# Second layer's gate moved from TensorE's last row set to VectorE in the feed-forward of an adaptive layer-norm block

## The chip, the cores and the metric

The kernel runs on one core of a Trainium2 chip. The metric is the device time of one execution in microseconds (us), the median of several runs. A core has five engines that work side by side and wait for one another through semaphores: TensorE (PE, matrix products; PEld are its weight loads), VectorE (DVE), ScalarE (ACT), GpSimd (POOL) and SyncE (SP, which here only starts DMA transfers; SPq and ACTq are the queues of SP and ACT).

## The reference

```python
x = L0_attn_data                                    # 2 batches x 512 rows x 512
mod = (_silu(L0_c) @ L0_wmod).reshape(2, 6, 1, -1)  # c: 2 x 512, wmod: 512 x 3072
sa, ca, ga, sb, cb, gb = (mod[:, 0], mod[:, 1], mod[:, 2], mod[:, 3], mod[:, 4], mod[:, 5])
ga = (2 * (ga >= 0) - 1) * jnp.maximum(jnp.abs(ga), 0.25)
gb = (2 * (gb >= 0) - 1) * jnp.maximum(jnp.abs(gb), 0.25)
h = _layernorm(x, axis=-1) * (1 + ca) + sa
x = x + ga * _L0_attn_ref(h, weight, mask)          # h @ (weight * block mask).T, 512 -> 512
h = _layernorm(x, axis=-1) * (1 + cb) + sb
x = x + gb * _L0_ffn_ref(h, Wg, Wu, Wd, ag, au, ad) # silu(h Wg.T * ag) * (h Wu.T * au), Wd.T, * ad; 512 -> 1376 -> 512
return x
```

The six vectors of `mod` (a shift, a scale and a gate for each of two layers, per batch) come from one small product with a 512 x 3072 matrix. The change is about the last of them, `gb`, the gate of the feed-forward.

## The kernel before

Everything is written out by hand: each engine has its own instruction stream, whose order is the order in the code, with a semaphore for every hand-over. The 1024 rows of x are 8 tiles of 128 rows (`n = 4 * b + t`, batch b, tile t).

**First layer.** VectorE takes means and variances of the tiles and normalises them; TensorE transposes them (`transposes`), ScalarE applies scale and shift (`modulate(n)`, n = 0..7), and TensorE multiplies with the masked weights: `linear(b, k, t)`, 32 products in all, k the inner quarter. The block mask is summed by VectorE (`sum_mask(k)`), spread by a small product (`mask_blocks(k)`), turned to 0/1 (`keep_blocks(k)`) and applied by GpSimd. Batch 1 of the first layer is normalised into a layout from which DMA moves (`move_first`, and `keep_in_place` for the blocks that stay) and VectorE's 32 x 32 transposes make the turned tiles.

**The modulation vectors** come in four sets, `rows_first`, `rows_second`, `rows_third`, `rows_last`. Each set (`mod_rows`) is a row of small products of `silu(c)` with weights in `modw`; ScalarE copies the result (`copy_rows`), TensorE turns it (`columns(n)`), and VectorE sums the columns out of the bank (`mod_columns`, `gate_sums`). The last set holds shift and scale of the second layer (slots 0 and 1 of `modw`) and the gate `gb` (slot 2). It stands in TensorE's stream behind `linear(1, 1, 1)`. Behind it stand the rest of the linears and `transposes(8)` to `transposes(11)`, which turn batch 0 of the second layer; `modulate(8)` to `modulate(11)` on ScalarE and `split` on VectorE make of each the high and low part that the feed-forward multiplies.

**Feed-forward.** It has STEPS = 22 steps, s = 0..21: 11 chunks of 128 inner features for batch 0, then the same for batch 1. A step has 16 products on TensorE (`gate_up(s)`, L935), a silu on ScalarE (L504), three operations on VectorE (`ffn_inner(s)`, L698, L705, L707) and 8 products (`down(s)`, L1005) two steps later. ScalarE also rounds each chunk's weights and, in the first steps, checks each chunk (`check_chunk(c)`, L442: is the low half of its words zero?). The results of the checks, in three groups of chunks, choose one of two product forms: `flag_vector(g)` on VectorE waits for the checks of group g, `flag_sum(g)` on TensorE adds them up, `read_flag(g)` brings the flag to a register. `flag_sum(2)` stands in TensorE's stream behind `gate_up(6)`, ahead of `down(4)`; `flag_vector(2)` stands on VectorE at the start of step 6. In steps 0 to 2 VectorE also normalises batch 1 of the second layer (`stats`, `normalise(3)`); 16 DMA moves and, in steps 5 to 8, `transpose_blocks` turn it.

**SP's queue** holds nearly all loads in one order: x, mask, weights of the first layer and the modulation, then the second layer's shift and scale (L294, L298, L300), its gate (L301, 1 MB), and then the chunks of the feed-forward, two transfers each (L308, L309). Chunks 0 to 3 follow at once; chunks 4 to 7 wait for `modulate(7)`; chunks 8 to 10 (from H1_CHUNK on) wait for the last linear, since their space holds the first layer's h.

**The second gate** before: `guard_gate(1)` in step 3 works on eight columns that `gate_sums(1)` took out of the bank, scales them with the down scale, and SP writes the turned line to DRAM and spreads it from there to all partitions (L324). It is wanted by `gate_ffn(0, 0)` on VectorE, when `down(10)` has made its first tile.

Of the kernel before, what the change touches and what calls it, by code (L numbers as in the profile page):

```python
# [25 lines left out]
ALU = mybir.AluOpType  # L26
# [4 lines left out]
P = 128  # L31
D = 512
KT = D // P
NB = 2
# [42 lines left out]
def adaln_block(nc, x, att_w, att_mask, cond, mod_ln1, mod_ln2, mod_gate, w_gu, w_gu_tail, w_down,  # L77
                scales, scales_tail, down_scale, out):
    with ExitStack() as ctx:
# [22 lines left out]
        gcol = sb("gcol", [P, 2, KT, NB])  # L102
        gscr = sb("gscr", [P, 2, KT, NB])
        gfin = sb("gfin", [P, 2, BLK])
        gturn = sb("gturn", [P, 2, BLK])
# [9 lines left out]
        colv = sb("colv", [P, 2, KT, NB])  # L115
# [69 lines left out]
        gcol_ok = sem("gcol_ok")  # L185
        gate_done = sem("gate_done")
        gate_ok = sem("gate_ok")
        gturn_ok = sem("gturn_ok")
        d_line = [sem(f"d_line{layer}") for layer in range(2)]
# [59 lines left out]
        def store_gate(eng, layer):  # L249

            eng.wait_ge(gturn_ok, layer + 1)
            line = gate_line[layer].rearrange("b k i -> (b k) i")
            for g in range(GRP):
                eng.dma_start(line[:, g * BLK:(g + 1) * BLK], gturn[BLK * g:BLK * g + NB * KT, layer, :])\
                   .then_inc(d_line[layer], 16)
# [5 lines left out]
        def _(sp):  # L261
# [59 lines left out]
            store_gate(sp, 1)  # L321
            sp.wait_ge(d_line[1], 16 * GRP)
# [61 lines left out]
        def _(act):  # L384
# [67 lines left out]
            def round_d(s):  # L452
# [22 lines left out]
            store_gate(act, 0)  # L475
# [5 lines left out]
               .then_inc(d_gate_first, 16)  # L481
            copy_rows(3)
            check_chunk(next(check_at))
# [39 lines left out]
        def _(dve):  # L523
# [3 lines left out]
            dve.memset(gfin[:, :, :], 0.0).then_inc(zeroed, 1)  # L527
# [98 lines left out]
            def gate_sums(layer):  # L626

                sum_columns(SETS - 2 + layer, bank[3 if layer else 7], GATE_AT, KT,
                            colv[:, layer, :, :].rearrange("p i b -> p (i b)")).then_inc(cols_ok, 1)
# [11 lines left out]
            def guard_gate(layer):  # L641


                dve.wait_ge(cols_ok, layer + 1)
                g = colv[:, layer, :, :]
                half_sign, gate = gscr[:, layer, :, :], gcol[:, layer, :, :]
                by_batch = gfin[:, layer, 0:NB * KT].rearrange("p (b k) -> p k b", b=NB)
# [7 lines left out]
                if layer == 0:  # L655
                    dve.wait_ge(zeroed, 4)
# [80 lines left out]
            for j in range(GRP):  # L737
                keep_in_place(j)
# [442 lines left out]
```

## Time and profile before

| | |
|---|---|
| median of 3 runs | 175.96 us (175.79 to 176.62) |
| the profiled execution | 176.29 us, span 174.5 us |
| mean granted TensorE clock | 0.999 |
| TensorE busy | 167.5 us, 96% |
| VectorE busy | 102.6 us, 59% |
| ScalarE busy | 80.9 us, 46% |
| GpSimd busy | 27.7 us, 16% |

The span reaches from the first to the last instruction of the profile; 1.79 us of the execution lie around it. Times in the profile are us from the span's start. A row of the timeline merges neighbouring instructions of one kind: its start, how long they took together, their number, and in brackets the idle time ahead of them with what ended it. One fp32 product with 512 columns stands as two records (two passes), one with 128 columns too, so the 48 products of `rows_last` are x96. A transfer's landing is its issue time plus the time to landing.

### The profile page before, as it was taken

The page shows a single profiled execution, that of the slowest core. Times are in us where ns is not written, and L with a number is a line of the kernel's source. Part 1 is how long each engine was busy: PE and PEld are TensorE (multiplying, and loading weights), DVE is VectorE, ACT ScalarE, POOL GpSimd, SP SyncE. Part 2 cuts the span into 40 slices and gives each one's busy share as a digit, 9 for nine tenths or more (in the row PEclk, how much of TensorE's full clock was granted, in tenths as well). Part 3 has the DMA queues.
Part 4 walks back from the last instruction along what each step waited for, and adds up shares of the span by engine and source line. Part 5 has one row for each costly group of instructions (what it writes and reads, how often), then busy time and mean ns, then how long its engine had stood idle before and what let it go on. Part 6 is the DMA issues. An engine that isn't in the chain of part 4 may idle for free.

```text
span 174.5 us, 2549 instructions
## 1 busy us (share of the span) xinstructions
PE 167.5 (96%) x892; PEld 128.4 (74%) x892; DVE 102.6 (59%) x216; ACT 80.9 (46%) x113; POOL 27.7 (16%) x32
## 2 busy tenths in 40 slices
PE   6889999979999999999999999999999999999992
PEld 6855554455468888888888888888888888888781
DVE  6778966990783999414855554437544313442574
ACT  3034005508999958755466442553425534252200
POOL 1233321930039310000000000007400000000000
PEclk9999999999999999999999999999999999999999
DMA  5999976999999501443000000001500000000014
GB/s 168 359 407 401 405 212 185 411 405 355 414 389 337 159 0 34 103 95 114 29 0 4 0 4 0 4 0 62 184 4 0 4 0 4 2 4 0 4 60 180
DMA packets 12789, 23.99 MB, mean 138 GB/s; under 512 B 3072, under 2 KB 5376, under 8 KB 12384
## 3 DMA queue, kind: packets, MB, share of 16 engines
q1 hardware_dynamic: 11056, 22.03, 35.1%
q10 hardware_dynamic: 1712, 1.66, 3.1%
q8 instruction: 16, 0.26, 0.6%
q14 instruction: 5, 0.04, 0.1%
HBM read 19.74 MB, written 2.11 MB: 125 GB/s over the span
## 4 chain that ended last, share of the span: by engine, by line
PE 80%; DMA 8%; DVE 5%; SPq 4%; issue 1%; ACT 0%; ACTq 0%
PE bank L935 46%; PE bank L1005 20%; PE bank L906 8%; DMA modw<-in_mod_gate 5%; DMA xt<-in_x 3%; SPq L246 3%; PE bank L813 2%; PE bank L991 2%; PE bank L885 2%; DVE wffn L576 1%; DVE xn L556 1%; DVE bns L542 1%; DVE xt L803 0%; SPq L263 0%; DVE xn L717 0%
## 5 line engine op out<-in xcount | busy, mean ns | idle before, releaser
L935 PE MATMUL bank<-ht,whi_gu 128*128 128x512 f32 x352 | 83.5, 391 | 0.0
L935 PEld LDWEIGHTS bank<-ht,whi_gu 128*128 128x128 f32 x352 | 65.6, 188 | 13.7 <-issue 0.5
L698 DVE SCALAR_TENSOR_TENSOR awork<-bank,scal,awork 128x512 f32<-128x512 f32 x22 | 16.5, 750 | 50.9 <-PE bank L935 47.6
L1005 PE MATMUL bank<-whi_dn,in_split 128*128 128x512 f32 x148 | 37.2, 391 | 0.0
L504 ACT ACTIVATE awork<-bank,scal 128x512 f32<-128x512 f32 x22 | 15.2, 689 | 45.3 <-PE bank L935 45.3
L1005 PEld LDWEIGHTS bank<-whi_dn,in_split 128*128 128x128 f32 x148 | 27.6, 188 | 6.0
L906 PE MATMUL bank<-awork,wffn 128*128 128x512 f32 x64 | 30.5, 603 | 0.2 <-ACT wffn L427 0.2
L449 ACT ACTIVATE whi_gu<-wffn 128x1024 fp32r<-128x1024 f32 x22 | 23.3, 1058 | 6.6 <-PE bank L935 6.6
L906 PEld LDWEIGHTS bank<-awork,wffn 128*128 128x128 f32 x64 | 11.0, 190 | 10.3 <-issue 9.0
L707 DVE TENSOR_TENSOR in_split<-awork,in_split 128x512 fp32r<-128x512 f32 x21 | 16.5, 785 | 0.7
L442 ACT ACTIVATE junk<-wffn 128x1536 uint8<-128x1536 uint16 x11 | 16.2, 1476 | 0.2
L379 POOL TENSOR_TENSOR xt<-xt,xn 128x512 f32<-128x512 f32 x4 | 5.2, 1346 | 54.5 <-DVE xn L717 54.5
L457 ACT ACTIVATE whi_dn<-wffn 128x512 fp32r<-128x512 f32 x21 | 13.1, 622 | 0.0
L542 DVE BATCH_NORM_STATS2 bns<-xt 128x6 f32<-128x512 f32 x16 | 10.8, 674 | 1.6 <-DMA xt<-in_x 1.5
L358 POOL TENSOR_TENSOR xt<-xt,xn 128x512 f32<-128x512 f32 x8 | 10.2, 1308 | 3.6 <-DVE xn L676 3.6
L402 ACT ACTIVATE rows<-bank,onerow 128x128 f32<-128x128 f32 x4 | 1.5, 368 | 19.9 <-PE bank L813 19.9
L705 DVE CAST in_split<-awork 128x512 fp32r<-128x512 f32 x21 | 9.0, 430 | 0.7
L345 POOL TENSOR_TENSOR rstd<-veps,mhalf 128x2 f32<-128x2 f32 x8 | 6.1, 763 | 15.2 <-DVE veps L547 15.1
L1074 PE MATMUL bank<-ident 128*128 128x128 f32 x34 | 6.6, 382 | 1.6 <-POOL ident L338 1.6
L1074 PEld LDWEIGHTS bank<-ident 128*128 128x128 f32 x34 | 6.4, 293 | 1.6 <-POOL ident L338 1.6
L813 PEld LDWEIGHTS bank<-modw,sc 128*32 128x32 f32 x192 | 5.0, 110 | 3.2 <-issue 3.2
L813 PE MATMUL bank<-modw,sc 128*32 128x128 f32 x192 | 6.1, 274 | 0.9 <-DMA modw<-in_mod_gate 0.9
(75 smaller groups left out, 109.6 us busy)
## 6 DMA issues: line engine op xcount, KB each, us to landing
wffn<-in_w_gu SPq DMA_DIRECT2D x10, 512.0 KB, 11.7
modw<-in_mod_ln SPq DMA_DIRECT2D x6, 512.0 KB, 7.1
wffn<-in_w_down SPq DMA_DIRECT2D x10, 256.0 KB, 13.1
xt<-in_x SPq DMA_DIRECT2D x8, 256.0 KB, 6.3
modw<-in_mod_gate SPq DMA_DIRECT2D x2, 1024.0 KB, 10.2
maskt<-in_att_mask SPq DMA_DIRECT2D x4, 256.0 KB, 8.0
awork<-in_att_w SPq DMA_DIRECT2D x4, 256.0 KB, 8.1
modw<-in_mod_ln SPq DMA_DIRECT2D x1, 1024.0 KB, 6.7
```

The lines of the kernel that those rows point to most:

```text
L442: act.activation(junk[:, :], low, ACT.Copy, accum_out=chk[:, c:c + 1])\
L449: act.activation(whi_gu[:, s % 2, :], wffn[:, s % C, 0:2 * D], ACT.Copy)\
L457: act.activation(whi_d(s), raw_d(s % C), ACT.Copy).then_inc(wd_hi, 1)
L504: act.activation(silu_g[:, s % 2, :], bank[gu_bank(s, 0)][:, :], ACT.Silu, scale=scal[:, s % C, 0:1]).then_inc(silu_ok, 1)
L542: dve.bn_stats(bns[:, q, t, :], xt[:, n % (NB * TT), :]).then_inc(bn_done, 1)
L698: dve.scalar_tensor_tensor(inner[:, s % 2, :], bank[gu_bank(s, 1)][:, :], scal[:, c, 1:2], silu_g[:, s % 2, :], ALU.mult, ALU.mult).then_i ...
L707: dve.tensor_tensor(lo, inner[:, s % 2, :], hi.bitcast(F32), ALU.subtract)\
L813: last = pe.matmul(dst[BLK * j:BLK * (j + 1), 0:P], sc[:, j, at * BLK:(at + 1) * BLK], source(j), start=(i == 0), stop=(i == len(blocks) - 1))
L906: last = pe.matmul(bank[4 * b + t][:, :], h1[:, b, k, t * P:(t + 1) * P], awork[:, k, :], start=(k == 0), stop=(k == KT - 1))
L935: return pe.matmul(bank[gu_bank(s, u)][:, :], w, h, start=(k == 0 and part == 0), stop=(k == KT - 1 and part == 1))
L1005: last = pe.matmul(bank[4 + t][:, :], h, w, start=(c == 0 and part == 0), stop=(c == C - 1 and part == 1))
L1074: pe.matmul(bank[0][:, 0:P], ident[:, :], ident[:, :], start=True, stop=True)
```

## The change

The gate `gb` leaves TensorE's last row set. Its 1 MB of weights is loaded behind the eighth chunk (chunk 7) instead of ahead of the first. VectorE makes the products itself in steps 3 and 4: for each batch one multiplication and three fused multiply-adds of 128 x 512 with a column of `silu(c)` (`second_gate_products`), turns them in step 5 with one 32 x 32 block transpose over 128 x 1024 and sums each block's row (`second_gate_sums`), and in step 9 folds the four partition groups together, guards, scales and turns the result (`guard_second_gate`, 14 small operations). SP stores one 32 x 32 line in one transfer instead of four. In TensorE's stream the last set has 32 products instead of 48, and `columns(3)`, the transposes 8 to 11 and `flag_sum(0)` stand one or a few linears earlier. On ScalarE one `check_chunk` moves from behind `copy_rows(3)` to ahead of it. On VectorE `sum_mask(3)` moves ahead of the four `keep_in_place`.

```diff
             sp.dma_start(modw[:, 1, :, :], mod_ln2[1]).then_inc(d_ln2[1], 16)
-            sp.dma_start(modw[:, 2, :, :], mod_gate[1]).then_inc(d_gate[1], 16)
...
                 if c == H1_CHUNK:
+                    sp.dma_start(modw[:, 2, :, :], mod_gate[1]).then_inc(d_gate[1], 16)
                     sp.wait_ge(att_done, NB * TT)
...
+            check_chunk(next(check_at))
             copy_rows(3)
             check_chunk(next(check_at))
-            check_chunk(next(check_at))
...
+            def second_gate_products(b):
+                dve.wait_ge(silu_c, 1)
+                dve.wait_ge(d_gate[1], 16)
+                for j in range(KT):
+                    w, c = modw[:, 2, j, :], sc[:, j, b:b + 1]
+                    if j == 0:
+                        dve.tensor_scalar(gates[:, b, :], w, c, None, ALU.mult).then_inc(gate2_part, 1)
+                    else:
+                        dve.wait_ge(gate2_part, KT * b + j)
+                        dve.scalar_tensor_tensor(gates[:, b, :], w, c, gates[:, b, :], ALU.mult, ALU.add)\
+                           .then_inc(gate2_part, 1)
+            def second_gate_sums():
+                dve.wait_ge(gate2_part, NB * KT)
+                turned = gates[:, NB:2 * NB, :].rearrange("p b n -> p (b n)")
+                dve.transpose(turned, gates[:, 0:NB, :].rearrange("p b n -> p (b n)")).then_inc(gate2_turned, 1)
+                dve.wait_ge(gate2_turned, 1)
+                dve.tensor_reduce(gsum[:, :], turned.rearrange("p (n i) -> p n i", i=BLK), AX_X, ALU.add)\
+                   .then_inc(gate2_sum, 1)
...
+            sum_mask(3)
             for j in range(GRP):
                 keep_in_place(j)
-            sum_mask(3)
...
             mod_columns(3)
-            gate_sums(1)
...
-                if s == 3:
-                    guard_gate(1)
+                if s in (3, 4):
+                    second_gate_products(s - 3)
                 if 5 <= s < 9:
                     transpose_blocks(s - 5)
+                if s == 5:
+                    second_gate_sums()
                 if 6 <= s < 10:
                     split(6 + s)
+                if s == 9:
+                    guard_second_gate()
...
-                pe.wait_ge(d_gate[1], 16)
                 pe.wait_ge(att_read, 3)
-                mod_rows([(KT * slot + i, modw_block(slot, i)) for slot in range(3) for i in range(KT)], bank[2])
+                mod_rows([(KT * slot + i, modw_block(slot, i)) for slot in range(2) for i in range(KT)], bank[2])
...
                     if (k, t) == (1, 1):
                         rows_last()
+                    if (k, t) == (1, 2):
+                        columns(SETS - 1)
                     if (k, t) == (1, 3):
-                        columns(SETS - 1)
-                    if (k, t) == (2, 0):
                         transposes(8)
                         transposes(9)
-                    if (k, t) == (2, 2):
+                    if (k, t) == (2, 0):
                         transposes(10)
                     if (k, t) == (2, 3):
                         transposes(11)
-                    if (k, t) == (3, 0):
                         pe.wait_ge(modc_ok, SETS)
                         flag_sum(0)
```

What the change makes of TensorE's stream between `linear(1, 1, 1)` and `flag_sum(0)` is seen in the next two lists. L906 and L980 are the linears, L813 and L888 the row set, L859 and L933 `columns(3)`, L885 and L959 the transposes 8 to 11. Before:

```order
L813 MATMUL bank<-modw,sc 32x128 [waits d_gate1,att_read,d_ln2_1,d_ln2_0]
L813 MATMUL bank<-modw,sc 32x128 x47
L906 MATMUL bank<-awork,wffn 128x512 x2
L859 MATMUL bank<-ident,rows 128x128 [waits att_read,rows_copied]
L906 MATMUL bank<-awork,wffn 128x512 [waits h_ok]
L885 MATMUL bank<-ident,xn 128x128 [waits att_read,xn_ok]
L885 MATMUL bank<-ident,xn 128x128 x3
L885 MATMUL bank<-ident,xn 128x128 [waits att_read]
L885 MATMUL bank<-ident,xn 128x128 x3
L906 MATMUL bank<-awork,wffn 128x512 x2
L885 MATMUL bank<-ident,xn 128x128 [waits h_ok]
```

And of the change:

```order
L888 MATMUL bank<-modw,sc 32x128 [waits att_read,d_ln2_1,d_ln2_0]
L888 MATMUL bank<-modw,sc 32x128 x31
L980 MATMUL bank<-awork,wffn 128x512
L933 MATMUL bank<-ident,rows 128x128 [waits att_read,rows_copied]
L980 MATMUL bank<-awork,wffn 128x512
L959 MATMUL bank<-ident,xn 128x128 [waits att_read,xn_ok]
L959 MATMUL bank<-ident,xn 128x128 x3
L959 MATMUL bank<-ident,xn 128x128 [waits att_read]
L959 MATMUL bank<-ident,xn 128x128 x3
L980 MATMUL bank<-awork,wffn 128x512 [waits h_ok]
L959 MATMUL bank<-ident,xn 128x128 [waits h_ok]
```

The wait for `d_gate1` and 16 products are gone; between the row set and `columns(3)` stands one linear instead of two, between it and the transposes 8 and 9 two instead of three, and between these and the transposes 10 one instead of two.

On ScalarE, around `copy_rows(3)` (L402, of the change L426), L442 and L466 are `check_chunk`, L430 and L454 `modulate`, L480 and L504 the spreading of the first gate. Before:

```order
L480 DMA maskt<-gate_line 128x512 [waits d_line0]
L402 ACTIVATE rows<-bank,onerow 128x128 [waits cols_done,rows_done]
L442 ACTIVATE junk,chk<-wffn 128x1536 [waits d_ffn0]
L442 ACTIVATE junk,chk<-wffn 128x1536 [waits checked,d_ffn1]
L430 ACTIVATE hbuf<-bank,modc 128x512 [waits modc_ok,xt_done] x2
```

And of the change:

```order
L504 DMA maskt<-gate_line 128x512 [waits d_line0]
L466 ACTIVATE junk,chk<-wffn 128x1536 [waits d_ffn0]
L426 ACTIVATE rows<-bank,onerow 128x128 [waits cols_done,rows_done]
L466 ACTIVATE junk,chk<-wffn 128x1536 [waits checked,d_ffn1]
L454 ACTIVATE hbuf<-bank,modc 128x512 [waits modc_ok,xt_done] x2
```

The check of chunk 0 now stands ahead of the copy, that of chunk 1 still ahead of `modulate(8)`.

On VectorE, the end of step 5 and the start of step 6, of the change (before, the rows L701 and L703 are not there, and L682 and L687 are the flag's two):

```order
L622 STREAM_TRANSPOSE xn<-modw 128x512 [waits d_blocks3,d_blocks2,xt_done,d_blocks1,d_blocks0]
L701 STREAM_TRANSPOSE maskt<-maskt 128x1024 [waits gate2_part]
L703 TENSOR_REDUCE gsum<-maskt 128x32 [waits gate2_turned]
L754 TENSOR_REDUCE flagv<-chk 128x1 [waits checked]
L759 TENSOR_SCALAR flags<-bank 1x1 [waits flag_done]
L770 SCALAR_TENSOR_TENSOR awork<-bank,scal,awork 128x512 [waits in_lo,silu_ok,up_mm]
```

Two operations over 1024 columns now stand between the block transpose of step 5 and `flag_vector(2)` (L754).

## Rows read from the trace of the kernel before

**Rows 1.** The page: busy time of TensorE.

```profile
PE 167.5 (96%) x892; PEld 128.4 (74%) x892; DVE 102.6 (59%) x216; ACT 80.9 (46%) x113; POOL 27.7 (16%) x32
```

**Rows 2.** The chain that ended last, in order of time: start, us, what.

```profile
27.86 8.81 DMA modw<-in_mod_gate
...
41.77 0.86 PE bank L906 x2
42.63 0.87 PE bank L885 x8
...
50.70 10.89 PE bank L935 x48
```

**Rows 3.** Timeline of TensorE from 32 to 66 us.

```profile
31.57 4.46 PE L906 MATMUL bank<-awork,wffn 128*128 128x512 f32 x10
36.91 2.83 PE L813 MATMUL bank<-modw,sc 128*32 128x128 f32 x96 [0.89 <-DMA modw<-in_mod_gate]
```

**Rows 4.** SP's timeline: when the transfers were issued.

```profile
10.36 0.43 SPq L266 DMA_DIRECT2D maskt<-in_att_mask  x1
...
27.35 0.46 SPq L300 DMA_DIRECT2D modw<-in_mod_ln  x1
...
29.12 0.68 SPq L309 DMA_DIRECT2D wffn<-in_w_down  x1
...
30.46 0.44 SPq L309 DMA_DIRECT2D wffn<-in_w_down  x1
```

**Rows 5.** DMA, one transfer each, last column us to landing; gate line last.

```profile
maskt<-in_att_mask SPq DMA_DIRECT2D x1, 256.0 KB, 12.2
modw<-in_mod_ln SPq DMA_DIRECT2D x1, 1024.0 KB, 6.7
wffn<-in_w_down SPq DMA_DIRECT2D x1, 256.0 KB, 9.5
wffn<-in_w_down SPq DMA_DIRECT2D x1, 256.0 KB, 11.1
maskt<-gate_line SPq DMA_DIRECT2D x1, 512.0 KB, 3.5
```

**Rows 6.** Timeline of all engines from 20 to 50 us.

```profile
21.91 1.77 DVE L582 COPY wffn<-wffn 32x512 f32<-32x512 f32 x4
23.71 0.69 DVE L603 TENSOR_REDUCE msum<-maskt 128x16 f32<-128x512 int32 x1
24.45 0.30 PEld L869 LDWEIGHTS bank<-msum,blkones 128*128 128x128 f32 x2 [0.29 <-DVE msum L603]
...
37.02 2.08 DVE L576 TENSOR_SCALAR xn<-xt,mv,rstd 128x512 f32<-128x512 f32 x4
39.80 0.37 ACT L402 ACTIVATE rows<-bank,onerow 128x128 f32<-128x128 f32 x1 [5.32 <-PE bank L813]
41.72 1.48 ACT L442 ACTIVATE junk<-wffn 128x1536 uint8<-128x1536 uint16 x1
43.20 1.43 ACT L430 ACTIVATE hbuf<-bank,modc 128x512 f32<-128x512 f32 x2
```

**Rows 7.** Timeline in the feed-forward, steps 0, 5 and 6.

```profile
56.24 1.67 DVE L707 TENSOR_TENSOR in_split<-awork,in_split 128x512 fp32r<-128x512 f32 x1
...
79.33 0.69 DVE L707 TENSOR_TENSOR in_split<-awork,in_split 128x512 fp32r<-128x512 f32 x1
79.94 0.71 DVE L598 STREAM_TRANSPOSE xn<-modw 128x512 f32<-128x512 f32 x1
80.57 0.12 DVE L682 TENSOR_REDUCE flagv<-chk 128x1 fp32r<-128x4 f32 x1
83.10 0.08 PEld L920 LDWEIGHTS bank<-onecol_r,flagv 128*1 128x1 f32 x1
```

**Rows 8.** One feed-forward step by windows: length, then each engine's busy time.

```profile
71.94:77.38 5.44, 5.44 (x25) 4.51 (x25) 1.87 (x3) 3.62 (x7) 0.00 (x0) 1.00 0.42 99
```

**Rows 9.** Groups of VectorE instructions by form: busy us, mean ns.

```profile
L665 DVE STREAM_TRANSPOSE gturn<-gfin 128x32 f32<-128x32 f32 x2 | 0.4, 213 | 0.1
```

More of the change, by code:

```diff
@@ L474, in _ @@
             modulate(4)
-            store_gate(act, 0)
+            store_first_gate(act)
             modulate(5)
@@ L658, in guard_gate @@
                    .then_inc(gate_m, 1)
-                dve.wait_ge(gate_m, layer + 1)
-                if layer == 1:
-                    dve.wait_ge(d_small, 48)
-                    dve.tensor_tensor(by_batch, gate, adc[:, :].unsqueeze(2).to_broadcast([P, KT, NB]),
-                                      ALU.mult).then_inc(gcol_ok, 1)
-                    dve.wait_ge(gcol_ok, 1)
-                dve.transpose(gturn[:, layer, :], gfin[:, layer, :]).then_inc(gturn_ok, 1)
+                dve.wait_ge(gate_m, 1)
@@ new lines, in second_gate_sums, with guard_second_gate @@
+            def second_gate_sums():
[5 more added lines that the diff above has]
+                   .then_inc(gate2_sum, 1)
+            def guard_second_gate():
+                own = slice(0, BLK)
+                dve.wait_ge(gate2_sum, 1)
+                dve.wait_ge(d_small, 48)
+                for q in range(GRP):
+                    dve.tensor_copy(adcf[own, :].rearrange("c (k q) -> c q k", q=GRP)[:, q, :],
+                                    adc[BLK * q:BLK * (q + 1), :]).then_inc(adc_fold, 1)
+                for q in range(GRP):
+                    dve.tensor_copy(gfold[own, q, :], gsum[BLK * q:BLK * (q + 1), :]).then_inc(gate2_fold, 1)
+                dve.wait_ge(gate2_fold, GRP)
+                dve.tensor_reduce(gval[own, :, :].rearrange("c b n -> c (b n)"),
+                                  gfold[own, :, :].rearrange("c q n -> c n q"), AX_X, ALU.add)\
+                   .then_inc(gate2_val, 1)
+                dve.wait_ge(gate2_val, 1)
+                dve.tensor_scalar(gsign[own, :, :], gval[own, :, :], 0.0, 0.5, ALU.is_ge, ALU.subtract)\
+                   .then_inc(gate2_sign, 1)
+                dve.wait_ge(gate2_sign, 1)
+                dve.scalar_tensor_tensor(gmag[own, :, :], gsign[own, :, :], 2.0, gval[own, :, :],
+                                         ALU.mult, ALU.mult).then_inc(gate2_mag, 1)
+                dve.wait_ge(gate2_mag, 1)
+                dve.scalar_tensor_tensor(gval[own, :, :], gmag[own, :, :], GATE_MIN, gsign[own, :, :],
+                                         ALU.max, ALU.mult).then_inc(gate2_guarded, 1)
+                dve.wait_ge(gate2_guarded, 1)
+                dve.wait_ge(adc_fold, GRP)
+                dve.tensor_tensor(gscaled[own, :, :], gval[own, :, :],
+                                  adcf[own, :].unsqueeze(1).to_broadcast([BLK, NB, NBLK]), ALU.mult)\
+                   .then_inc(gate2_scaled, 1)
+                dve.wait_ge(gate2_scaled, 1)
+                dve.transpose(gline[own, :], gscaled[own, :, :].rearrange("c b n -> c (b n)"))\
+                   .then_inc(gline_ok, 1)
```

87 lines of the change are left out of this document (53 added, 34 removed).

## The prediction

> **What bounds the kernel now.** I read the page first: TensorE is busy for 167.5 of 174.5 us [rows 1]. So the time can only change by what TensorE executes and by the few microseconds in which it stands. The chain that ended last says where it stands: it runs through TensorE from 36.91 us to nearly the end, and ahead of that through one transfer, the second gate's weights, issued at 27.86 and landed at 36.67 [rows 2]. TensorE's timeline shows the same from the other side: ten linears in a row end at 31.57 + 4.46 = 36.03 us, then 0.89 us of waiting for that transfer, then the last row set for 2.83 us, until 39.74 [rows 3]. From there to the first product of the feed-forward at 50.70 [rows 2] are 10.96 us in which TensorE hardly pauses. The feed-forward runs in steps of 5.44 us in which TensorE is busy for 5.44, VectorE for 1.87 and ScalarE for 3.62 [rows 8]. Work added to VectorE there costs nothing unless TensorE waits for it.
>
> **The change part by part.**
>
> *The row set.* 16 of 48 products leave. They are alike, so 2.83 x 16/48 = 0.94 us leave TensorE's stream.
>
> *The wait.* Without the gate, the last transfer that the set waits for is the second layer's other 1 MB: issued at 27.35 [rows 4], 6.7 us to landing [rows 5], so at 34.05. TensorE comes at 36.03: 2 us later. The whole 0.89 us go. Together 1.83 us: TensorE is through with the set at 36.03 + 1.89 = 37.92 instead of 39.74.
>
> *Where the waiting could go to.* From 37.92 on everything TensorE wants comes 1.83 us earlier, and some of it is also moved ahead in its stream. I follow each.
> The copy of the rows on ScalarE is wanted after one linear (0.86 us [rows 2]) instead of two, at 38.78. It takes 0.37 and started 0.06 us behind the set [rows 6], so it is ready at 38.35 if ScalarE is free. But the check of chunk 0 stands ahead of it now. ScalarE had 5.32 us of idle time there [rows 6], and a check takes 1.48 (41.72 to 43.20 [rows 6]). It can't begin before chunk 0 is there. Before, that was 29.12 + 9.5 = 38.6 us [rows 4, 5]; now 1 MB less lies ahead of it. What 1 MB takes in this queue is read from two landings, 36.67 - 34.05 = 2.62 us. So chunk 0 lands at 36.0. Chunk 1 landed at 30.46 + 11.1 = 41.56 [rows 4, 5] and its check began at 41.72: 0.16 us later. The check of chunk 0 so runs from 36.2 to 37.7, ahead of the 37.98 at which the copy can start. Nothing is lost until chunk 0 lands 0.7 us later than I reckon: 0.3 until the copy is late, and 0.4 of slack behind the copy.
> Transposes 8 and 9 are wanted after one more linear, at 39.75 with the turning of the columns. The normalised tiles they read are ready at 37.02 + 2.08 = 39.10 [rows 6], an edge that doesn't move with the change. 0.65 us are left of it.
> Transposes 10 need `modulate(8)`, which stands on ScalarE behind the check of chunk 1. Chunk 1 lands at 41.56 - 2.62 = 38.94, the check ends at 38.94 + 0.16 + 1.48 = 40.58, `modulate(8)` (half of 1.43 [rows 6]) at 41.3. TensorE wants it at 39.75 + 0.87 (transposes 8, 9 [rows 2]) + 0.86 = 41.48. 0.2 us are left: the tightest place in this stretch, and it is paced by a transfer. Then three linears follow (2.6 us) in which ScalarE can check chunk 2 and make `modulate(9)` and `(10)`. Cost of the moved pieces: 0, and 0.5 if chunk 1 comes 0.7 later.
>
> *The mask sum moved up.* TensorE's weight load for the last mask product waited 0.29 us for it [rows 6], and this edge lies ahead on TensorE's path. Moved ahead of four copies (1.77 us, from 21.91 [rows 6]), the sum would be early by that; but its mask lands only at 10.36 + 12.2 = 22.6 us [rows 4, 5], so it runs to 23.25 and the copies end at 25.0. Between 0 and 0.29 us are won here. But a TensorE that is 0.29 us earlier wants `modulate(8)` at 41.2, ahead of the 41.3 above, since that is paced by chunk 1. So most of it ends in that wait. I take 0.05.
>
> *VectorE in steps 3 and 4.* Four operations of 128 x 512 for each batch: one at 0.52 (2.08 / 4 [rows 6]) and three at 0.69 [rows 7], 2.6 us a step. With its own 1.87 that makes 4.5 of 5.44 [rows 8]: covered. The weights land behind chunk 7, long ahead of step 3. What waits for `ffn_inner` is a product of the step after next.
>
> *VectorE in step 5.* Here is the one place where TensorE can meet the new work. `flag_sum(2)` stands ahead of `down(4)` in TensorE's stream, and waits for `flag_vector(2)`, which now stands behind a transpose and a sum over 1024 columns. Before, the block transpose ended at 80.57, when the flag's own 0.12 us began, and TensorE loaded the flag at 83.10 [rows 7]: 2.4 us of slack behind the flag. The trace has no operation over 1024 columns. From below, by the slope: a transpose of 32 columns takes 0.213 [rows 9], one of 512 0.71 [rows 7], so 1.03 ns a column and 1.23 us for 1024; the sum took 0.69 for 512 [rows 6], with the same slope 1.21. Together 2.44, and the flag is ready at 83.13: TensorE waits for 0.03 to 0.1. From above, by doubling: 1.42 + 1.38 = 2.80, and TensorE waits for about 0.45. I take 0.1: both forms stream their columns, and a fixed part is paid once.
> The Trainium skill (VectorE: DVE Perf Modes, "The TRN2 errata") gives (N + 151) / 0.96 ns for an fp32 operation of two tensors and N columns, and its table of perf modes keeps `tensor_reduce` at that single rate. An estimate from that page is 1.22 us for each of the two, 2.45 together, and would make the sum what the slope makes it; by doubling, the forecast would be 0.35 us longer.
>
> *VectorE in step 9, and the line.* 14 operations of at most 32 columns, each near the 0.213 us of the small transpose [rows 9]: 3 us, beside 1.87 and a split (two operations, the larger at 0.69 [rows 7]). Step 9 then runs over its 5.44 by about 0.6, which step 10 takes up. By steps of 5.44 from the end of the first three at 50.70 + 10.89 [rows 2], `down(10)` begins at 116.0 in times of before; the line is ready about 107, its store is bounded by the spreading, 3.5 us [rows 5], and both are over at 114. Nothing waits. The four small stores and five small operations that go cost nothing before.
>
> *The sum.* 0.94 + 0.89 + 0.05 - 0.1 = 1.78 us. The profiled execution took 176.29 with a span of 174.5; I expect 174.5 and 172.7. The median, 0.33 us below the profiled execution, goes from 175.96 to 174.2.
>
> **The rivals.**
>
> *The chunks don't come earlier by the whole 2.62 us* (chance 0.15). The first gate's 256 KB share the queues from 35.7 us on, and ScalarE's order now has two checks tied to landings. Each 0.1 us beyond the slack at `modulate(8)` (0.2) or at the copy (0.7) is lost. If chunk 1 comes 1 us later than reckoned, 0.8 is lost: 175.0. For it: chunk 1 landed 3 us behind chunk 0 before. Against: the transfers are bound by bandwidth in that stretch, and 1 MB less is 1 MB less.
>
> *The two wide operations are slower than by doubling* (0.08), a transpose that writes beside what it reads in one tile. With 4 us together TensorE waits 1.6: 175.7.
>
> *The wait was a hidden one, and the time returns at another edge* (0.08): the normalised tiles (0.65 us of slack) or the split parts of the second layer late by 1.5 us ahead of the feed-forward, so that only the 16 products less remain, and of these half: 175.5, within 0.5%. The trace shows no wait of TensorE behind 39.74 that could grow so.
>
> *Slower: VectorE falls behind in steps 3 to 5* (0.05). One operation of two tensors took 1.67 us instead of 0.69 while GpSimd worked beside it [rows 7]. If the six fused operations took that, steps 3 and 4 would be 1.87 + 0.52 + 5.0 = 7.4 us each, 2.0 over 5.44, and `flag_vector(2)` 4 us later; TensorE would lose 4 and gain 1.8: 178.2. It decides from 1.9 us of lateness at the flag. Against it: GpSimd has nothing to do there (0.00 busy [rows 8]).
>
> *More is won* (0.04): the 0.29 us of the mask stay, and the flag costs nothing: 173.8.
>
> **How the numbers follow.** My forecast (0.6) spans 173.9 to 174.7: the flag between 0 and 0.45, the mask between 0 and 0.29, and 0.1 of measurement on either side. The range reaches to the rivals of late chunks and takes in the far end above: 173.7 to 175.2, which leaves out slow wide operations, the returned wait and the slower case, about 2 in 10. A change of under 0.5% (0.88 us) can't be told from none here. Faster by more than that are my forecast, the last rival and most of the late chunks, 0.85 with what lies between the cases; within it 0.1; slower 0.05.
>
> **What the profile after would show.** The row set as x64 with some 1.9 us and no wait for a transfer ahead of it; its end near 37.9. A check on ScalarE between 36 and 38, ahead of the copy. The first feed-forward product near 48.9. In step 5 a transpose and a sum of 1.2 us each, and TensorE's load of the third flag at most 0.1 us late. The forecast is wrong if TensorE shows a wait over 0.3 us for ScalarE's `modulate(8)` or the copied rows, or for the flag's reduction, or if the steps of the feed-forward are longer than 5.44.

## The result and the profile after

The changed kernel takes 174.88 us (median of 10 runs, 174.44 to 175.43), the kernel before 176.16 in the same measurement: the ratio is 0.9927, with a 95% interval of 0.991 to 0.9943. That is 1.28 us less where 1.78 were forecast (174.2). The time lies inside the range given, 173.7 to 175.2, and outside the narrower forecast in it, 173.9 to 174.7. The profiled execution took 175.16 us with a span of 173.4, against 176.29 and 174.5 before: 1.1 us less in the traces that follow.

The page of the changed kernel: TensorE is busy for 1.0 us less than before [rows 1], VectorE for 9.1 us more, and TensorE still fills 96% of the span.

```profile
PE 166.5 (96%) x860; PEld 126.7 (73%) x860; DVE 111.7 (64%) x234; ACT 80.9 (47%) x113; POOL 27.8 (16%) x32
```

The chain that ended last, of the changed kernel, in order of time (start, us, what; L980 linears, L888 row sets, L1009 and L1079 the products of the feed-forward):

```profile
22.81 1.47 PE bank L888 x48
...
25.55 0.44 issue
25.99 0.30 PE bank L933
...
36.49 1.89 PE bank L888 x64
38.38 1.06 PE bank L980 x2
...
49.34 10.92 PE bank L1009 x48
...
78.52 3.62 PE bank L1009 x16
82.15 0.11 issue
82.26 2.11 PE bank L1079 x8
84.37 3.63 PE bank L1009 x16
```

Four numbers are to be read here. The last row set is 1.89 us instead of 2.83 [rows 3], and no transfer stands ahead of it. It begins at 36.49; the linears before had ended at 36.03 [rows 3], so it comes 0.46 us late. From its end at 38.38 to the feed-forward at 49.34 are 10.96 us, to the hundredth what they were. And from the end of the products of step 6 (82.15) to the end of those behind the third flag (84.37) are 2.22 us; before it was 1.94, as the chain of that trace has it:

```profile
83.49 1.94 PE bank L1005 x8
```

The account is closed: 0.94 + 0.89 - 0.46 - 0.28 = 1.09 us of the 1.1 between the spans.

**Where 0.46 us went: the mask sum.** VectorE's timeline of the changed kernel, around the third row set:

```profile
23.32 0.69 DVE L627 TENSOR_REDUCE msum<-maskt 128x16 f32<-128x512 int32 x1 [1.88 <-DMA maskt<-in_att_mask]
23.93 1.76 DVE L606 COPY wffn<-wffn 32x512 f32<-32x512 f32 x4
25.72 0.17 DVE L632 TENSOR_SCALAR keep<-bank 128x16 f32<-128x16 f32 x1
26.33 0.17 DVE L639 TENSOR_REDUCE modc<-bank 128x4 f32<-128x16 f32 x1 [0.44 <-PE bank L933]
```

VectorE stood 1.88 us for the mask (issued at 10.33 and 13.0 us to landing in this trace, so landed at 23.3), began the sum hardly earlier than before (23.32 instead of 23.71 [rows 6]), and then the four copies of 1.76 us lay between the sum and `keep_blocks(3)` (L632), which turns TensorE's answer to 0/1. It came at 25.72. Before, with the copies ahead of the sum, it stood at 24.89. TensorE's turning of the third set's columns waits for it in the code: that is the 0.44 us of "issue" in the chain ahead of 25.99.

**Where 0.28 us went: the third flag.** The timeline of the changed kernel in steps 5 and 6, VectorE's rows and those of TensorE's weight loads (PEld; L994 is the flag's, L1079 the first product's behind it):

```profile
78.60 0.70 DVE L622 STREAM_TRANSPOSE xn<-modw 128x512 f32<-128x512 f32 x1
79.23 1.20 DVE L701 STREAM_TRANSPOSE maskt<-maskt 128x1024 f32<-128x1024 f32 x1
80.46 1.22 DVE L703 TENSOR_REDUCE gsum<-maskt 128x32 f32<-128x1024 f32 x1
81.60 0.15 DVE L754 TENSOR_REDUCE flagv<-chk 128x1 fp32r<-128x4 f32 x1
81.80 0.08 PEld L994 LDWEIGHTS bank<-onecol_r,flagv 128*1 128x1 f32 x1
82.26 1.68 PEld L1079 LDWEIGHTS bank<-whi_dn,in_split 128*128 128x128 f32 x8 [0.38 <-issue]
```

The two wide operations take 1.20 and 1.22 us. The flag is ready at 81.75 and TensorE loads it at 81.80. Those 0.05 us are no slack: in all seven traces with both wide operations ahead of the flag (this one and six of those told of below), the load comes 0.05 or 0.06 us behind the end of the flag's reduction, also in the two where the profile names the flag as what TensorE waited for. So I read it as a wait for the flag, if a short one: the load is 0.35 us ahead of the end of step 6's products (82.15), where it was 0.39 ahead before (83.10 [rows 7] and 83.49). It is 0.04 us late. But the next load comes 0.46 us behind the flag's, where it was 0.23 before:

```profile
83.33 1.68 PEld L1005 LDWEIGHTS bank<-whi_dn,in_split 128*128 128x128 f32 x8
```

Between the two loads stand, in TensorE's stream, two waits for data and the branch that chooses the product form.

**ScalarE's part held.** Its timeline in the changed kernel: check of chunk 0, the copied rows, check of chunk 1, `modulate(8)` and `(9)`.

```profile
35.97 1.48 ACT L466 ACTIVATE junk<-wffn 128x1536 uint8<-128x1536 uint16 x1 [1.02 <-DMA wffn<-in_w_down]
...
38.44 0.37 ACT L426 ACTIVATE rows<-bank,onerow 128x128 f32<-128x128 f32 x1 [0.90 <-PE bank L888]
38.71 1.47 ACT L466 ACTIVATE junk<-wffn 128x1536 uint8<-128x1536 uint16 x1
...
40.88 1.45 ACT L454 ACTIVATE hbuf<-bank,modc 128x512 f32<-128x512 f32 x2 [0.60 <-PE bank L959]
```

Here ScalarE waits for TensorE, twice, and not the other way round.

### The profile page after: what moved, and what is told of

The parts are those of the page before. It is cut to its first block, busy times and chain, and to the rows that moved or that the text cites. A ratio compares the mean times of both kernels' runs of the same rounds, so it can differ in the third digit from the quotient of the medians.

```text
span 173.4 us, 2502 instructions
## 1 busy us (share of the span) xinstructions
PE 166.5 (96%) x860; PEld 126.7 (73%) x860; DVE 111.7 (64%) x234; ACT 80.9 (47%) x113; POOL 27.8 (16%) x32
## 3 DMA queue, kind: packets, MB, share of 16 engines
HBM read 19.74 MB, written 2.11 MB: 126 GB/s over the span
## 4 chain that ended last, share of the span: by engine, by line
PE 90%; DMA 4%; SPq 2%; DVE 2%; issue 1%
PE bank L1009 46%; PE bank L1079 20%; PE bank L980 17%; DMA modw<-in_mod_ln 4%; PE bank L888 3%; PE bank L1065 2%; PE bank L959 2%; SPq L287 1%; SPq L293 1%; DVE xt L878 0%; DVE xn L789 0%; DVE xt L869 0%; DVE xn L875 0%; PE bank L943 0%; PE bank L933 0%
## 5 line engine op out<-in xcount | busy, mean ns | idle before, releaser
L1009 PE MATMUL bank<-ht,whi_gu 128*128 128x512 f32 x352 | 83.5, 391 | 0.0
L1009 PEld LDWEIGHTS bank<-ht,whi_gu 128*128 128x128 f32 x352 | 65.6, 188 | 13.8 <-issue 0.5
L1079 PE MATMUL bank<-whi_dn,in_split 128*128 128x512 f32 x148 | 37.2, 391 | 0.1
L1079 PEld LDWEIGHTS bank<-whi_dn,in_split 128*128 128x128 f32 x148 | 27.6, 188 | 6.2 <-issue 0.4
L980 PE MATMUL bank<-awork,wffn 128*128 128x512 f32 x64 | 30.6, 604 | 0.2 <-DMA modw<-in_mod_ln 0.2
L473 ACT ACTIVATE whi_gu<-wffn 128x1024 fp32r<-128x1024 f32 x22 | 23.3, 1058 | 6.6 <-PE bank L1009 6.6
L980 PEld LDWEIGHTS bank<-awork,wffn 128*128 128x128 f32 x64 | 11.0, 190 | 10.9 <-issue 9.5
L466 ACT ACTIVATE junk<-wffn 128x1536 uint8<-128x1536 uint16 x11 | 16.2, 1476 | 1.1 <-DMA wffn<-in_w_down 1.0
L426 ACT ACTIVATE rows<-bank,onerow 128x128 f32<-128x128 f32 x4 | 1.5, 368 | 15.3 <-PE bank L888 15.3
L1148 PE MATMUL bank<-ident 128*128 128x128 f32 x34 | 5.8, 350 | 1.6 <-POOL ident L362 1.6
L1148 PEld LDWEIGHTS bank<-ident 128*128 128x128 f32 x34 | 5.6, 263 | 1.6 <-POOL ident L362 1.6
L1065 PEld LDWEIGHTS bank<-whi_dn,in_split 128*128 128x128 f32 x40 | 5.9, 189 | 0.6
L376 POOL TENSOR_TENSOR awork<-awork,keep 128x512 f32<-128x512 f32 x4 | 4.4, 1110 | 11.3 <-DVE keep L632 11.3
```

Of the source, the lines that this page charges most:

```text
L466: act.activation(junk[:, :], low, ACT.Copy, accum_out=chk[:, c:c + 1])\
L473: act.activation(whi_gu[:, s % 2, :], wffn[:, s % C, 0:2 * D], ACT.Copy)\
L980: last = pe.matmul(bank[4 * b + t][:, :], h1[:, b, k, t * P:(t + 1) * P], awork[:, k, :], start=(k == 0), stop=(k == KT - 1))
L1009: return pe.matmul(bank[gu_bank(s, u)][:, :], w, h, start=(k == 0 and part == 0), stop=(k == KT - 1 and part == 1))
L1079: last = pe.matmul(bank[4 + t][:, :], h, w, start=(c == 0 and part == 0), stop=(c == C - 1 and part == 1))
L1148: pe.matmul(bank[0][:, 0:P], ident[:, :], ident[:, :], start=True, stop=True)
```

## The experiments

Times are medians beside the kernel before on the same chip; ratios are to the kernel before, with 95% intervals. "Third set to last set" is, in one trace, the time from the start of the third row set to the start of the last; "flag stretch" the time from the end of the products of step 6 to the end of those behind the flag (1.94 without loss). One execution of each kernel was profiled; the medians are over four to twelve, so a number from a trace need not be that of the median.

### The mask sum back behind the copies

```diff
-            sum_mask(3)
             for j in range(GRP):
                 keep_in_place(j)
+            sum_mask(3)
```

> The changed kernel with the mask sum back behind the four copies; all else as changed. My theory: moved up, the sum waited 1.88 us for its mask and pushed the copies and the 0/1 blocks behind them late, which held the turned columns (0.44 us of idle TensorE) and cost the row set 0.46 us (36.49 instead of 36.03). Then this kernel is 0.4 to 0.5 us faster than the changed one: some 174.4 us, ratio to before near 0.990, and the row set begins at 36.0. The rival, that the later start is a difference of this one trace (the mask landed later in it), expects the time of the changed kernel, 174.9 and 0.993.

Measured: 174.99 us, ratio 0.9922 (0.9902 to 0.9942), the time of the changed kernel. By the time, my expectation fell. In the chain of this kernel the mechanism is there and the gain lost:

```profile
23.18 1.45 PE bank L888 x48
...
36.17 1.89 PE bank L888 x64
...
78.20 3.63 PE bank L1009 x16
81.82 0.09 PE bank L994
81.92 0.29 issue
82.21 2.11 PE bank L1079 x8
84.32 3.63 PE bank L1009 x16
```

Third set to last set is 12.99 us instead of 13.68. But the flag stretch is now 2.50 instead of 2.22, and everything began 0.37 us later in this execution. The timeline says why the flag is not earlier though TensorE is:

```profile
78.54 0.71 DVE L622 STREAM_TRANSPOSE xn<-modw 128x512 f32<-128x512 f32 x1 [0.18 <-DMA modw<-modw]
...
81.75 0.08 PEld L994 LDWEIGHTS bank<-onecol_r,flagv 128*1 128x1 f32 x1 [0.35 <-DVE flagv L754]
```

The block transpose ahead of the wide operations waited for its 16 DMA moves. It had waited for them neither before nor in the changed kernel's trace. So the flag was ready only 0.05 us earlier (81.70), while TensorE was through with step 6 0.33 us earlier (81.82), and waited: that is 0.28 of the 0.69 us won at the mask. The other 0.37 lie ahead of the third set, where this edit changes nothing; one trace can't say whether that is more than the spread of executions.

### The wide operations behind the flag

```diff
-                if s == 5:
+                if s == 6:
                     second_gate_sums()
```

> The changed kernel with the wide transpose and sum in step 6, behind the third flag, instead of step 5. My theory: the flag's reduction ended at 81.75 where TensorE loaded it at 81.80, and the product behind came 0.28 us later than before, since TensorE's stream stood at the flag and could not run ahead to the branch behind it. Then this is 0.25 to 0.3 us faster than the changed kernel, some 174.6 us, and the stretch from the end of the products of step 6 to the end of those behind the flag is 1.94 us instead of 2.22. The rival, that VectorE's added work slows the feed-forward wherever it stands, expects the 0.28 us at another place and 174.9.

Measured: 174.61 us (173.81 to 176.09), ratio 0.9895 (0.9871 to 0.9918). The flag stretch is 1.94 (83.31 to 85.25). The loss is gone, and the steps stay at 5.44 us, so it comes at no other place. The profiled execution is the slowest of its seven; its clock is told of at the end.

### Both

```diff
-            sum_mask(3)
             for j in range(GRP):
                 keep_in_place(j)
+            sum_mask(3)
...
-                if s == 5:
+                if s == 6:
                     second_gate_sums()
```

> The changed kernel with both of these: mask sum behind the copies, wide operations behind the flag. If the two losses are apart and all that is lost, the sum is 0.94 + 0.89 = 1.83 us against before: some 174.3 us, ratio 0.9896. If a transfer paces the stretch behind the row set as soon as it begins 0.46 us earlier (modulate 8 behind the check of chunk 1), only a part of the first comes through: 174.5 or more.

Measured: 174.19 us (174.14 to 174.36), ratio 0.9882 (0.9861 to 0.9903), span 172.5. The chain:

```profile
22.91 1.45 PE bank L888 x48
...
35.90 1.89 PE bank L888 x64
...
48.74 10.92 PE bank L1009 x48
...
81.55 1.94 PE bank L1079 x8
```

12.99, 1.94, and from the row set's end at 37.79 to 48.74 10.95 us: both losses are gone and no transfer paces the stretch. The median is 1.99 us below that of before, against 1.83 by the two terms; the rest is within the interval.

### Only the mask sum moved up, in the kernel before

```diff
+            sum_mask(3)
             for j in range(GRP):
                 keep_in_place(j)
-            sum_mask(3)
```

> The kernel before with only the mask sum moved ahead of the four copies. My theory: the linears end about 0.46 us later, but the row set there waits 0.89 us for the gate's weights, so the time is that of before, 176.2 us (0 to 0.1 more), and the wait shrinks to 0.4. The rival, that the moved sum costs its 0.46 us by itself in any kernel, expects 176.6. That it wins time expects under 176.

Measured: 176.34 us, ratio 1.0012 (0.9993 to 1.003). In its chain the linears end at 36.07 and only 0.24 us remain until the row set:

```profile
28.34 7.73 PE bank L906 x18
36.07 0.24 issue
36.31 2.83 PE bank L813 x96
```

From the third set (22.59) to the end of the linears are 13.48 us instead of 13.12 (22.91 to 36.03). In the kernel before, the late blocks would have hidden in the wait for the gate's weights; the change takes that wait away and adds the late blocks in one go.

### The gate's weights ahead of the chunks again

```diff
             sp.dma_start(modw[:, 1, :, :], mod_ln2[1]).then_inc(d_ln2[1], 16)
+            sp.dma_start(modw[:, 2, :, :], mod_gate[1]).then_inc(d_gate[1], 16)
...
                 if c == H1_CHUNK:
-                    sp.dma_start(modw[:, 2, :, :], mod_gate[1]).then_inc(d_gate[1], 16)
                     sp.wait_ge(att_done, NB * TT)
```

> The changed kernel with the gate's 1 MB loaded ahead of chunk 0, as before; TensorE still doesn't wait for it. This parts the wait that left from the load that moved. My theory: chunk 0 lands near 38.6 again, its check (now ahead of the copy) ends at 40.2, the copied rows come at 40.6 where TensorE wants them at 39.3, and modulate 8 behind the check of chunk 1 comes near 43.9 where it is wanted at 42: about 2 us are lost against the changed kernel, 176.5 to 177. The rival, that leaving out the wait and the 16 products is what counts and where the load stands is hidden, expects 174.9.

Measured: four executions, 176.8, 178.34, 179.52 and 179.63 us, with before at 176.15 (175.61 to 176.89). The first had a mean granted clock of 1.00, the others 0.99. All are above every execution of the changed kernel (at most 175.49); the first is not above the range of the kernel before. That one lies inside what was expected (176.5 to 177), the others above it. The one profiled is that of 178.34 us. In it ScalarE begins the check at 38.79, and TensorE waits for the copied rows:

```profile
40.68 0.40 PE L933 MATMUL bank<-ident,rows 128*128 128x128 f32 x1 [1.76 <-ACT rows L426]
```

The direction and the place are as expected, but more is lost than that in this execution. The windows of this kernel (length, then busy time of TensorE, its weight loads, VectorE, ScalarE and GpSimd, the granted clock, DMA) show it:

```profile
38.00:40.60 2.60, 0.92 (x2) 0.09 (x1) 1.00 (x2) 1.81 (x3) 0.01 (x1) 1.00 1.00 397
40.60:42.60 2.00, 1.92 (x4) 0.79 (x5) 0.23 (x1) 0.92 (x2) 0.00 (x0) 0.55 0.99 336
42.60:44.30 1.70, 1.70 (x10) 1.70 (x9) 0.00 (x0) 1.30 (x3) 0.00 (x0) 0.52 1.04 410
44.30:46.00 1.70, 1.70 (x9) 0.94 (x9) 1.46 (x3) 1.69 (x3) 0.00 (x0) 1.00 1.01 404
```

After the idle stretch TensorE's granted clock stands at 0.55 and 0.52, near the lower of its two levels (1.2 of 2.4 GHz), for some 3.7 us; the transposes 8 and 9 take 1.64 us there instead of 0.87. The wait costs 1.8 us and the clock behind it about as much again: two records of a linear in 1.71 us instead of 0.86, and the transposes' 0.77, are 1.6. The execution of 176.8 us is 1.9 above the changed kernel's median: about the wait alone.

### The check of chunk 0 back behind the copy

```diff
-            check_chunk(next(check_at))
             copy_rows(3)
             check_chunk(next(check_at))
+            check_chunk(next(check_at))
```

> The changed kernel with the check of chunk 0 back behind the copy of the rows, so two checks stand ahead of modulate 8. Theory: copy at 38.8, two checks until 41.8, modulate 8 until 42.5, wanted by TensorE at 41.9 at the latest: 0.5 to 0.8 us lost, 175.4 to 175.7. The rival, that ScalarE has slack enough here, expects 174.9.

Measured: 175.38 us, ratio 0.9963 (0.9939 to 0.9987): 0.3 to 0.5 us more than the changed kernel in its two measurements (175.05 and 174.88), with intervals that overlap. TensorE's timeline has the wait where it was reckoned:

```profile
42.05 0.66 PE L959 MATMUL bank<-ident,xn 128*128 128x128 f32 x4 [0.53 <-ACT hbuf L454]
```

From the row set to the feed-forward are 11.66 us (37.80 to 49.46) instead of 10.96. In the traces the check's move was worth that 0.7. Here, too, the flag took a part: the stretch was 2.55 us (82.26 to 84.81), with the block transpose 0.32 us late by its DMA moves. The mask landed early in this trace, which gave 0.45 back.

### TensorE's old order behind the row set

```diff
-                    if (k, t) == (1, 2):
-                        columns(SETS - 1)
                     if (k, t) == (1, 3):
+                        columns(SETS - 1)
+                    if (k, t) == (2, 0):
                         transposes(8)
                         transposes(9)
-                    if (k, t) == (2, 0):
+                    if (k, t) == (2, 2):
                         transposes(10)
                     if (k, t) == (2, 3):
                         transposes(11)
+                    if (k, t) == (3, 0):
                         pe.wait_ge(modc_ok, SETS)
```

> The changed kernel with TensorE's order of before behind the row set (columns, transposes 8 to 11 and the first flag sum at their old places). Theory: nothing waits behind the row set with or without the move, 10.96 us from its end to the feed-forward in both kernels, so 174.9, within 0.2. The rival: the later transposes make the split parts late for the first products of the feed-forward, or the first flag late for the branch, and up to 1 us is lost.

Measured: 174.81 us, ratio 0.9918 (0.9886 to 0.9951); 10.97 us (38.28 to 49.25) from the row set to the feed-forward. In the trace the moved columns and transposes neither bring nor cost anything, and the time shows none either, within 0.6 us either way.

### The mask sum ahead of the last copy

```diff
-            sum_mask(3)
-            for j in range(GRP):
+            for j in range(GRP - 1):
                 keep_in_place(j)
+            sum_mask(3)
+            keep_in_place(GRP - 1)
```

(and the wide operations in step 6)

> As the kernel with both mends, but the mask sum stands ahead of the last of the four copies. The mask lands at 22.6 to 23.4, three copies end at 23.25, the sum at 23.9 to 24.1, ahead of the 24.2 at which TensorE wants it; the 0/1 blocks come when TensorE has made them, near 24.7. If the idea of the moved sum was right and only its place wrong, 0.2 to 0.3 us less than with the sum behind all four: some 174.0. If the 0.29 us that TensorE waited are taken up by the next edge (turned columns to modulated rows), no difference: 174.3.

Measured: 174.08 us (173.55 to 175.39), ratio 0.9887 (0.9852 to 0.9922); third set to last set 12.94 us (22.68 to 35.62) instead of 12.99. The sum was early enough (22.91) and 0.05 us came of it in the trace, and the times can't be told apart from those of the kernel with both mends: I could find nothing to win with the moved sum even at this place.

### The changed kernel again, the wide transpose alone, and 48 products

> The changed kernel as it is, beside the next two on one chip. 174.9 as in its first runs; the row set 13.5 to 13.7 us behind the start of the third set, and 2.2 us or more from the end of the products of step 6 to the end of those behind the third flag.

Measured: 175.05 us, ratio 0.9946 (0.9926 to 0.9966); flag stretch 2.16 (81.90 to 84.06), just under the 2.2 expected. But third set to last set was 13.15 (23.11 to 36.26): expected were 13.5 to 13.7.

In the next kernel `second_gate_sums` holds the wide transpose alone, `second_gate_rest` the sum.

```diff
                 if s == 5:
                     second_gate_sums()
+                if s == 6:
+                    second_gate_rest()
```

> The changed kernel with the wide transpose left in step 5 and only the sum (1.22 us) moved behind the flag, into step 6. The flag is then ready some 1.2 us ahead of TensorE's load instead of 0.05. If what TensorE lacked was only the lead over the branch behind the flag (0.3 to 0.4 us seen), the stretch is 1.94 us as before and the kernel takes 174.6. If TensorE needs a lead of more than 1.2 us there, part of the 0.28 stays.

Measured: 174.27 us, ratio 0.9896 (0.9878 to 0.9914); flag stretch 1.94 (81.60 is the end of step 6's products):

```profile
79.81 0.12 DVE L756 TENSOR_REDUCE flagv<-chk 128x1 fp32r<-128x4 f32 x1
...
81.60 1.94 PE bank L1083 x8
```

A flag that is ready at 79.93, 1.3 us ahead of its load at 81.21, costs nothing. On the same chip as the changed kernel, the intervals don't overlap: so this one move is a gain in the measured times, too. It is larger there (0.78 us) than the 0.22 at the flag; 0.29 us lie ahead of the third set, which began at 22.82 here and at 23.11 there. With the 0.03 between the third and the last set these make 0.54 of the 0.57 us between the two profiled executions (174.33 and 174.90); why the medians are 0.2 further apart stays open.

```diff
+                    sp.wait_ge(rows_done, SETS)
                     sp.dma_start(modw[:, 2, :, :], mod_gate[1]).then_inc(d_gate[1], 16)
...
-                mod_rows([(KT * slot + i, modw_block(slot, i)) for slot in range(2) for i in range(KT)], bank[2])
+                mod_rows([(KT * slot + i, modw_block(slot, i)) for slot in range(3) for i in range(KT)], bank[2])
```

> The changed kernel with 48 products in the last row set again, the 16 added ones reading the first gate's weights, which lie there already (their result is not used); no wait for a transfer comes back. This parts the products from the wait. Theory: the row set takes 2.83 us again, all else shifts with it, 174.9 + 0.94 = 175.8. The rival, that a wait behind the set takes up part of it (TensorE would wait there anyway when it comes earlier), expects less than 0.7 us more.

Measured: 175.76 us, ratio 0.9976 (0.995 to 1.0001): 0.71 us more than the changed kernel beside it, hardly more than the 0.7 under which the rival would have stood; the time alone doesn't part the two. The traces do. The row set takes 2.76 us (it ends at 39.04, the feed-forward begins at 50.00, 10.96 later), so 0.87 us are the products' in the trace, and nothing behind them takes any of it back.

## Why the prediction was right, and where its sizes were off

**The products and the wait: right.** The row set shrank by 0.94 us, and with 48 products it takes 0.87 more at unchanged surroundings. No transfer is waited for. With both later losses mended, the last row set stands within 0.13 us of where these two terms put it (35.90 to 37.79, forecast 36.03 to 37.92).

**The transfer that moved: right, and the condition of the rest.** Chunk 0's check began at 35.97, forecast for 36.2. Chunk 1 landed at 37.9 (issued at 29.51, 8.4 us to landing), forecast for 38.94, and its check began right behind the copy, at 38.71: so `modulate(8)` was not the tight place that I took it for, with 0.2 us left. ScalarE stood ready for it and waited 0.60 us for TensorE. The rival of late chunks had its place right: with the gate's load put back, 1.76 us of waiting come there, nearly the whole of the 1.83 forecast for the products and the wait, and in the profiled execution the clock's cost comes on top.

**Moving the check: right**, put at no cost; undone, two checks in a row stand ahead of `modulate(8)` and cost 0.7 us there in the trace. **Moving columns and transposes: right**, at nothing.

**The mask sum: wrong, in size and sign.** The step was "Between 0 and 0.29 us are won here. [...] I take 0.05", and it lost 0.46 us in the profiled execution against the one before, 0.69 against the kernels with the sum behind the copies. I had reckoned that the mask lands at 22.6 and the copies end at 25.0, and looked only at what waits for the sum. What stands behind the copies on VectorE, `keep_blocks(3)`, and who waits for it, I did not follow. The traces show how the loss depends on the mask's landing, 23.3 us in the first trace of the changed kernel and not 22.6. With the sum moved up, by how long it begins after the third set's start on TensorE:

| kernel | sum begins, against third set | third set to last set |
|---|---|---|
| old TensorE order | +0.57 | 13.72 |
| changed | +0.51 | 13.68 |
| before, mask up | +0.32 | 13.48 |
| check behind | +0.08 | 13.23 |
| changed again | -0.02 | 13.15 |
| transpose alone | -0.05 | 13.12 |
| 48 products | -0.10 | 13.07 |
| gate's weights ahead | about -0.1 | 13.05 |
| wide operations behind | -1.24 | 12.94 |
| sum behind all copies (2 kernels) | | 12.99 |

Down to 13.07 it falls one for one with the sum's start, from 0.7 us of loss to 0.1, and then it levels off: at 1.24 us ahead there are 0.05 us of gain and no more. (For the kernel before, the last column ends with the linears; the chain of the kernel with the gate's weights ahead doesn't run through these sets, so its row is from the timeline.) The landing is a matter of the single execution. So in the traces this is shown, and it is why the first trace of the changed kernel has 0.69 us of loss and the second 0.16. With the landing that I had reckoned, 0.2 us ahead of the third set, next to nothing would have been lost by this table: the step failed by what it left out, and how much that costs is for each execution's landing to say. In the measured times the loss is not shown: with the flag mended, the sum ahead of all four copies gave 0.9895 and 0.9896, behind them 0.9882, ahead of the last one 0.9887, and these intervals overlap.

**The flag: the wait was right, what it costs was not.** The term was 0.1 us for a TensorE that waits 0.03 to 0.1; it measured 0.28 and 0.22 in the two traces of the changed kernel, and 0.56 and 0.61 in two of the variants. The durations by the slope were right: 1.20 and 1.22 us for 1.23 and 1.21. An estimate by the formula of the Trainium skill (VectorE: DVE Perf Modes, "The TRN2 errata") for an operation of two tensors is 1.22 us for each: the trace agrees for the sum, for which the page's table gives the single rate. The lateness of the flag's load was right as well, 0.04 and 0.05 us. What I left out were two things. The products behind the flag come later than the flag by more than its lateness: in the seven traces with both wide operations ahead of it, the load is 0.04 to 0.46 us later against the end of step 6's products than without loss, and the products are 0.15 to 0.24 us later than that, since the next load comes 0.36 to 0.46 us behind the flag's instead of 0.22 or 0.23. It shows in the second trace of the changed kernel, too:

```profile
81.36 0.15 DVE L754 TENSOR_REDUCE flagv<-chk 128x1 fp32r<-128x4 f32 x1
81.56 0.08 PEld L994 LDWEIGHTS bank<-onecol_r,flagv 128*1 128x1 f32 x1
81.94 1.69 PEld L1079 LDWEIGHTS bank<-whi_dn,in_split 128*128 128x128 f32 x8 [0.29 <-issue]
```

My reading is that TensorE's sequencer can't run ahead to the branch while the flag is waited for, and so pays for the branch in the open. No run takes the branch away, so this is argued and not shown. A flag that is ready 1.3 us ahead of its load costs nothing; what lies between wasn't tried. And the start of VectorE's chain is bound to 16 DMA moves, which in two variants landed 0.18 and 0.32 us after VectorE wanted them, so that a TensorE that comes earlier finds the flag no earlier. This is a part of why mending the mask alone gave nothing, 0.28 us in that trace.

**The rest of the rivals.** VectorE's added work in steps 3, 4 and 9 cost nothing, and the steps stayed at 5.44 us. Slower wide operations didn't come. Of the signs that I had named for a wrong forecast, none is there: TensorE waits for neither the copied rows nor `modulate(8)`, the products behind the flag are 0.28 us late, under the 0.3, and the steps without a flag take 5.44 us. But the places that I had named are late by what the mask sum cost: the row set ends at 38.38 and not near 37.9, the feed-forward begins at 49.34 and not near 48.9. The range held by luck in part: its lower part was for more won and its upper for late chunks, and what filled it was the mask and the flag, while the chunks came early.

The kernel with both mends took 174.19 us. The one that also moves the sum ahead of the last copy (174.08) and the one with only the wide sum behind the flag (174.27) can't be told from it. That 174.2 was forecast for the change itself is a coincidence of two terms that nearly cancel in the sum, +0.05 and -0.1.

## What to carry to other kernels

When an instruction that may wait for a transfer is moved up in an engine's stream, follow not only who wants its result but everything that now stands behind it, and take the landing with its spread from trace to trace, not as a number. When a wait on the path is removed, list what it hid, for the same change may hold both. And give a semaphore that an engine meets just ahead of its next piece of work a lead: here a flag 0.04 us late cost 0.28 us, and one 1.3 us early nothing.

## What the runs showed of the hardware

TensorE's clock fell after an idle stretch of 1.76 us in the middle of full work (granted 1.00 ahead of it, 0.55 and 0.52 behind it), and cost about as much again as the wait. The 0.89 us of waiting before the change had no such effect: the granted clock in the windows behind it is 1.00. Another profiled execution, that of the wide operations behind the flag, had a granted clock of 0.72 between 8 and 14 us, behind an idle stretch of 1.74 us, and its third row set began at 24.73 instead of some 22.9; it was the slowest of its seven runs by 1.1 us. But the length of the stretch alone doesn't decide it: the kernel with both mends stood for 1.77 us at the same place, from 7.03 to 8.80, and its granted clock was 1.00 there and behind it.

A semaphore that came 0.04 us too late for TensorE to keep its pace cost 0.28 us: 0.11 us of standing TensorE in the chain, and the rest within the first products behind, whose eight took 2.11 us instead of 1.94. From the end of VectorE's reduction to the load that waits for it are 0.05 or 0.06 us in all seven traces.
